# The joined last two attention layers: one order of TensorE by blocks of four heads, four shared PSUM banks, stacks made four heads at a time

## What is computed

```python
# layer 2: 16 heads of 16, keys and values from the normalised context
a = layernorm(ctx) * gamma + beta
Q, K, V = x @ Wq.T, a @ Wk.T, a @ Wv.T
attn = softmax(where(mask, Q K^T * 16 ** -0.5, -inf))
x = x + tanh(gate) * ((attn V) @ Wo.T)
# layer 3: 32 query heads of 8 on 8 key heads, then a layer norm
q, k, v = x @ Wq + bq, ctx @ Wk + bk, ctx @ Wv + bv
attn = softmax(q k^T * 8 ** -0.5 + mask)
x = layernorm((attn v) @ Wo + bo + x) * gamma + beta
```

## Time and profile before

| | us |
|---|---|
| median of three runs | 1309.61 (1308.80 to 1310.96) |
| the profiled execution, timed | 1311.66 |
| its span in the profile | 1309.9 |
| layers 0 and 1, within the span | 0 to 945 |
| layers 2 and 3 | 945 to 1309.9 |

### The profile page before, as it was taken

One profiled execution on the slowest core, in us unless ns is written; L12 is line 12 of the kernel. 1 busy time (PEld: TensorE's weight loads), 2 busy tenths in 40 slices (PEclk: granted clock), 3 DMA queues, 4 the chain that ended last, 5 costly groups with the idle time before them and its releaser, 6 DMA issues. The chain is left out here.

```text
span 1309.9 us, 20641 instructions
## 1 busy us (share of the span) xinstructions
PE 1165.3 (89%) x7388; PEld 897.3 (68%) x7388; DVE 831.0 (63%) x2027; ACT 634.9 (48%) x1420; POOL 678.7 (52%) x735
## 2 busy tenths in 40 slices
PE   5999999999999999999989669874788888899996
PEld 4788888888888888888878624433554556566664
DVE  6776666766757666667666456985554445566764
ACT  3655655555655555555652215103244444566663
POOL 3665665657655665566753032850136433456664
PEclk9999999999999999999999879997889999999999
DMA  6210221102211122102202000000010000000000
GB/s 204 65 49 17 65 65 52 58 21 65 66 49 39 44 65 65 48 18 65 65 17 80 17 0 1 1 0 1 22 43 26 2 1 1 1 2 10 2 10 17
DMA packets 35109, 47.04 MB, mean 36 GB/s; under 512 B 3865, under 2 KB 22082, under 8 KB 35010
## 3 DMA queue, kind: packets, MB, share of 16 engines
q1 hardware_dynamic: 34640, 44.83, 10.8%
q10 hardware_dynamic: 370, 0.91, 0.2%
HBM read 44.69 MB, written 1.05 MB: 35 GB/s over the span
## 5 line engine op out<-in xcount | busy, mean ns | idle before, releaser
L444 POOL TENSOR_TENSOR a_prob<-a_prob,a_inv_total 128x512 f32<-128x512 f32 x128 | 144.1, 1126 | 208.3 <-DVE a_inv_total L732 208.3
L1962 POOL TENSOR_TENSOR scores<-scores,neg_max 128x512 f32<-128x512 f32 x144 | 147.7, 1040 | 160.5 <-DVE neg_max L1833 160.5
L637 ACT ACTIVATE a_prob<-psum,a_neg_max 128x257 f32<-128x257 f32 x256 | 118.9, 472 | 94.1 <-DVE a_neg_max L729 93.3
L1758 ACT ACTIVATE prob_T<-psum 128x512 f32<-128x512 f32 x192 | 110.2, 591 | 75.7 <-PE psum L1677 75.2
L1677 PE MATMUL psum<-ident,scores 128*128 128x128 f32 x768 | 116.9, 285 | 9.8 <-POOL scores L1962 8.2
L1677 PEld LDWEIGHTS psum<-ident,scores 128*128 128x128 f32 x768 | 85.7, 144 | 47.3 <-issue 22.9
L1833 DVE CUSTOM_DVE_ANT_0 scores<-psum,ctx_rows 128x256 f32<-128x256 f32 x256 | 93.0, 419 | 25.6 <-PE psum L1661 25.4
L736 DVE TENSOR_TENSOR a_probT_lo<-psum,a_probT_hi 128x512 fp32r<-128x512 f32 x128 | 88.0, 687 | 32.6 <-ACT a_probT_hi L641 32.1
L566 PE MATMUL psum<-ident,a_prob 128*128 128x128 f32 x512 | 77.8, 274 | 24.0 <-DVE a_probT_lo L736 21.6
L566 PEld LDWEIGHTS psum<-ident,a_prob 128*128 128x128 f32 x512 | 60.0, 140 | 44.6 <-issue 20.8
L729 DVE TENSOR_REDUCE a_neg_max<-psum 128x2 f32<-128x514 f32 x128 | 87.2, 681 | 1.2 <-PE psum L486 1.2
(11 more groups left out here) (348 smaller groups left out, 3349.4 us busy)
## 6 DMA issues: line engine op xcount, KB each, us to landing
wk_raw<-in_L_xattn_wk SPq DMA_DIRECT2D x16, 512.0 KB, 6.5
wq_raw<-in_L_xattn_wq SPq DMA_DIRECT2D x16, 512.0 KB, 5.7
wv_raw<-in_L_xattn_wv SPq DMA_DIRECT2D x16, 512.0 KB, 3.7
wo_raw<-in_L_xattn_wo SPq DMA_DIRECT2D x16, 512.0 KB, 3.9
ctx_rows<-in_ctx SPq DMA_DIRECT2D x3, 512.0 KB, 4.4
x_rows<-in_x SPq DMA_DIRECT2D x2, 512.0 KB, 9.6
ctx_rows<-in_mask_Bx1xSxS_ff SPq DMA_DIRECT2D x1, 1024.0 KB, 5.6
out_dram<-x_rows SPq DMA_DIRECT2D x4, 256.0 KB, 2.1
```

Of the source, the lines that this page charges most:

```text
L444: pool.tensor_tensor(prob[:, m % 4, :, 0:S], prob[:, m % 4, :, 0:S], rtot[:, m % 4, :].unsqueeze(2).to_broadcast([P, 2, S]), ALU.mult)
L637: act.activation(prob[:, m % 4, q, 0:S + 1], s_bank(g)[:, q, 0:S + 1], ACT.Exp, bias=negm[:, m % 4, q:q + 1], accum_out=tot[:, m % 4, q:q ...
L1758: act.activation(pT[:, i % PT, :], t_bank(i), ACT.Exp, scale=1.0 if on_scalar(i) else -1.0).then_inc(exp_ok, 1)
L1962: pool.tensor_tensor(sc[:, i % SC, :, :], sc[:, i % SC, :, :], m[:, i % SC, :].unsqueeze(2).to_broadcast([P, 2, S]), ALU.subtract).then_in ...
```

## The change

- TensorE takes four turns (each with its piece), then two pairs of scores, then the sums of the four heads before: T F T F T F T F S S A. The pairs are those of heads i + 5 to i + 8, so the scores run up to eight heads ahead.
- Turns, sums and pieces share banks 4 to 7 in a ring, in the order of their use; each waits for whoever read that bank before (`bank_read`).
- Stacks are made for four heads at a time (`stack_pieces`), and a block's scores wait only for the stacks of their four heads. The opening ahead of the first scores holds two of them; the others, and the V pieces, stand behind turns. The places of all pieces change; in layer 3 they are two in four turns, later one in three.
- The eviction of the piece behind turn i stands after the maximum of head i + 3 (`LEAD`). The stacks of layer 3's second slot are all evicted by ScalarE.
- The keep of the sums comes one block later. The scale of layer 2's Q is applied in its eviction, and GpSimd no longer scales the weight. GpSimd's side work is cut smaller and spread; its scale and offset of finished rows are two steps, two heads apart.

```diff
+LEAD = 3
-F_BANK = 7
...
-def slot_pieces(l, h):
-    sh = SMALL[l]
-    return ([('Q', l, h, c) for c in range(NC)] + [('K', l, h, c) for c in range(sh.KC)] + [('V', l, h, n) for n in range(2 if l == 2 else 1)]
-            + [('SQ', l, h, g) for g in range(sh.G)] + [('SK', l, h, g) for g in range(8)])
+def stack_pieces(l, h, g):
+    return [('SQ', l, h, g), ('SK', l, h, g)] + ([('SK', l, h, 4 + g)] if l == 2 else [])
...
-    opening = [('XT2', 0, c) for c in range(NC)] + [('CT', 0, c) for c in range(NC)] + [('Q', 2, 0, c) for c in range(NC)]
-    opening += [('XT2', 1, c) for c in range(NC)] + [('AT', 0, c) for c in range(NC)] + [('K', 2, 0, c) for c in range(NC)]
-    opening += [('SQ', 2, 0, g) for g in range(4)] + [('SK', 2, 0, g) for g in range(8)]
-    second = [('V', 2, 0, 0), ('V', 2, 0, 1), ('AT', 1, 0), ('AT', 1, 1)]
+    opening = [('XT2', 0, c) for c in range(NC)] + [('CT', 0, c) for c in range(NC)] + [('Q', 2, 0, 0)] + [('AT', 0, c) for c in range(NC)]
+    opening += [('Q', 2, 0, 1), ('K', 2, 0, 0)] + stack_pieces(2, 0, 0) + stack_pieces(2, 0, 1)
+    second = [('XT2', 1, 0), ('XT2', 1, 1), ('AT', 1, 0), ('AT', 1, 1), ('K', 2, 0, 1)]
     behind = {}
...
-    put(0, [('CT', 1, c) for c in range(NC)] + [('Q', 2, 1, c) for c in range(NC)] + [('K', 2, 1, c) for c in range(NC)]
-        + [('SQ', 2, 1, g) for g in range(4)] + [('SK', 2, 1, g) for g in range(8)] + [('V', 2, 1, n) for n in range(2)])
-    put(20, output_pieces(2, 0) + [('XT3', 0), ('K', 3, 0, 0)])
-    put(28, [('SK', 3, 0, g) for g in range(7)])
-    put(35, output_pieces(2, 1) + [('XT3', 1), ('SK', 3, 0, 7)] + [('Q', 3, 0, c) for c in range(NC)]
-        + [('SQ', 3, 0, g) for g in range(8)] + [('V', 3, 0, 0)])
...
+    put(0, stack_pieces(2, 0, 2) + [('V', 2, 0, 0), ('V', 2, 0, 1)] + stack_pieces(2, 0, 3))
+    put(8, [(kind, 2, 1, c) for kind in 'QK' for c in range(NC)] + [('CT', 1, 0), ('CT', 1, 1)] + stack_pieces(2, 1, 0) + stack_pieces(2, 1, 1))
+    put(20, stack_pieces(2, 1, 2)[:1] + output_pieces(2, 0) + [('XT3', 0)] + stack_pieces(2, 1, 2)[1:] + stack_pieces(2, 1, 3) + [('V', 2, 1, 0), ('V', 2, 1, 1)]
+        + [('K', 3, 0, 0), ('SK', 3, 0, 0)])
+    put(36, [('SK', 3, 0, 1)] + output_pieces(2, 1) + [('XT3', 1), ('Q', 3, 0, 0), ('Q', 3, 0, 1), ('SQ', 3, 0, 0), ('SQ', 3, 0, 1), ('V', 3, 0, 0)]
+        + stack_pieces(3, 0, 2) + stack_pieces(3, 0, 3)[:1])
+    put(53, output_pieces(2, 2) + [('XT3', 2)] + stack_pieces(3, 0, 3)[1:] + [p for g in range(4, 8) for p in stack_pieces(3, 0, g)])
+    put(69, output_pieces(2, 3) + [('XT3', 3), ('K', 3, 1, 0), ('Q', 3, 1, 0), ('Q', 3, 1, 1)]
+        + [(kind, 3, 1, g) for kind in ('SK', 'SQ') for g in range(8)] + [('V', 3, 1, 0)] + output_pieces(3, 0), 2)
+    put(134, output_pieces(3, 1), 3)
+    put(165, output_pieces(3, 2) + output_pieces(3, 3)[:2], 3)
-    bank = {p: k % 8 for k, p in enumerate(opening)}
-    bank.update(zip(second, (7, 6, 4, 5)))
-    bank.update({p: F_BANK for p in behind.values()})
-    bank.update(zip(ending, (7, 0, 1, 2)))
-
-    pe = [('F', p) for p in opening] + [('S', 0), ('S', 1)] + [('F', p) for p in second]
+    pe = [('F', p) for p in opening] + [('S', 0), ('S', 1)] + [('F', p) for p in second] + [('S', 2), ('S', 3)]
     for i in range(HEADS):
         pe.append(('T', i))
         if i in behind:
             pe.append(('F', behind[i]))
-        if i % 2 and i // 2 + 2 < HEADS // 2:
-            pe.append(('S', i // 2 + 2))
-        if i % 4 == 1 and i > 4:
-            pe.append(('A', i // 4 - 1))
+        if i % 4 == 3:
+            pe += [('S', s) for s in (i // 2 + 3, i // 2 + 4) if s < HEADS // 2]
+            if i > 4:
+                pe.append(('A', i // 4 - 1))
     pe += [('A', QUADS - 1)] + [('F', p) for p in ending]
+
+
+    bank, earlier, held, ring = {}, {}, {}, 0
+    for kind, p in pe:
+        if kind != 'S':
+            if kind == 'F' and p in opening:
+                b = opening.index(p) % 8
+            else:
+                b = 4 + ring % 4
+                ring += 1
+            bank[kind, p], earlier[kind, p] = b, held.get(b)
+            held[b] = (kind, p)
...
-        if kind == 'S' and p == 1:
+        if kind == 'S' and p == 2:
             act.append(('shift', 2))
         if kind == 'T':
             at = p
             act.append(('exp', p))
+            if p % 4 == 0 and p > 4:
+                act.append(('keep', p // 4 - 2))
         if kind == 'A' and p == QUADS - 1:
             at = HEADS
-            act.append(('keep', p))
+            act += [('keep', p - 1), ('keep', p)]
         if kind == 'F':
-            if p == ('SQ', 2, 0, 0):
+            if p == ('V', 2, 0, 0):
                 act.append(('gate', 0))
-                dve.append(('mask', 0))
             if evictor(p) == 'act' or p[0] in 'QK':
                 act.append(('E', p))
             if evictor(p) == 'dve':
-                if p[0] == 'V' and p[1:3] == (2, 0):
-                    max_to(1 + p[3])
+                if p == ('K', 2, 0, 1):
+                    max_to(1)
                 elif at >= 0:
-                    max_to(at + 2)
+                    max_to(at + LEAD)
                 dve.append(('E', p))
-                if p == ('Q', 2, 0, 1):
-                    dve.append(('normalise', 1))
+                if p == ('Q', 2, 0, 0):
+                    dve += [('mask', 0), ('normalise', 1)]
                 if p[:2] == ('OP', 3):
                     dve.append(('moments', p[2]))
             if at % 4 == 3 and at + 3 < HEADS:
                 act.append(('shift', at + 3))
-            if at % 4 == 2 and at > 4:
-                act.append(('keep', at // 4 - 1))
-    return pe, act, dve, bank, behind
+    return pe, act, dve, bank, earlier, behind
...
     if p[0] in ('SQ', 'SK'):
-        return 'act' if p[3] % 2 == 0 else 'dve'
+        return 'act' if p[3] % 2 == 0 or p[1:3] == (3, 1) else 'dve'
...
+                def bank_read(use):
+
+                    if earlier[use]:
+                        kind, what = earlier[use]
+                        if kind == 'F':
+                            landed(pe, [what])
+                        else:
+                            pe.wait_ge(exp_ok if kind == 'T' else kept, what + 1)
...
-                    if s == 0:
-                        landed(pe, [p for p in number if number[p] < number['V', 2, 0, 0]])
-                    elif e == 0 and b % 2 == 0:
-                        landed(pe, slot_pieces(l, b // 2))
+                    if s < 2:
+                        pieces = [p for (kind, p), bank in bank_of.items() if kind == 'F' and bank < 4]
+                        landed(pe, [max((p for p in pieces if evictor(p) == who), key=number.get) for who in ('act', 'dve')])
+                    if e % 4 == 0 and b % 2 == 0:
+                        landed(pe, stack_pieces(l, b // 2, e // 4))
...
-                    if i < 2:
-                        landed(pe, [('AT', 1, i)])
-                    else:
-                        pe.wait_ge(exp_ok, i - 1)
+                    bank_read(('T', i))
...
-                            act.activation(dst, src[0:r, :], ACT.Copy).then_inc(hi_ok, 1)
+                            act.activation(dst, src[0:r, :], ACT.Identity, scale=-SMALL[2].scale if kind == 'Q' else 1.0).then_inc(hi_ok, 1)
...
                 def extras(i):
+                    if i == 4:
+                        set_ones(2, 1).then_inc(ones, 1)
+                    if i == 6:
+                        clear(spare[1].bitcast(F32))
                     if i == 8:
                         pool.wait_ge(ld['q3'], 16)
                         pool.tensor_scalar(w3['q'][:, :, :], w3['q'][:, :, :], -SMALL[3].scale, None, ALU.mult).then_inc(scaled, 1)
+                    if i == 10:
                         pool.tensor_scalar(nq[:, :].unsqueeze(2), chip.vecs[:, :, VROWS['L3_xattn_bq']:VROWS['L3_xattn_bq'] + 1], -SMALL[3].scale, None, ALU.mult).then_inc(bias_ok, 1)
-                    if i == 12:
-                        pool.wait_ge(ld['mask3'], 16)
-                        pool.tensor_scalar(mask3[:, 0:4, :], mask3[:, 0:4, :], -1.0, None, ALU.mult)
-                    if i == 14:
-                        pool.tensor_scalar(mask3[:, 4:8, :], mask3[:, 4:8, :], -1.0, None, ALU.mult).then_inc(mask_ok, 1)
-                    if i == position['V', 2, 1, 1] + 3:
-                        made(pool, ('V', 2, 1, 1))
+                        clear(selq[3][:].rearrange("p a g j r w -> p (a g j r w)").bitcast(F32))
+                    for k in range(4):
+                        if i == 12 + 2 * k:
+                            choose_keys(k)
+                        if i == 24 + 2 * k:
+                            choose_queries(k)
+                        if i == 40 + 3 * k:
+                            pool.wait_ge(ld['mask3'], 16)
+                            two = mask3[:, 2 * k:2 * k + 2, :]
+                            pool.tensor_scalar(two, two, -1.0, None, ALU.mult).then_inc(mask_ok, 1)
```

(53 more changed lines are left out.)

45 lines of the change are left out of this document (23 added, 22 removed).

## The result

The changed kernel is slower: 1327.5 us median (1320.9 to 1328.32) against 1309.84 (1308.8 to 1310.96) for the kernel before on the same chip, a ratio of 1.0128 with a 95% interval of 1.0097 to 1.0159. Forecast were 1297.8, and at most 1319. Its profiled execution took 1320.9 us, span 1318.9.

A forecast was written before the change was run, and what follows sets the result against it. TensorE's order was taken as the limit. Turn 0 at 966.3 plus blocks of 317.4 gave last sums at 1283.7 against 1295.47, 11.8 us less; from a median of 1309.61 that made 1297.8 us, range 1268 to 1319.

The forecast's parts named there:

- The opening: Ahead of turn 0: fewer pieces and no scaling of Wq put turn 0 at 966.3, 11.1 us earlier.
- rival 3: Half-clock stretch and VectorE's queue hold the first scores: turn 0 at 975, 1307 to 1310 us, no change; chance 0.09.
- The waits that go: TensorE's waits for bank 7's eviction (9.0 us) and GpSimd's subtraction (8.2 us) vanish, not counted beside the blocks.
- The ring: Banks 4 to 7 shared by turns, sums and pieces: turns' waits for their bank costed at nothing.
- The chain: Heads' blocks: second pair waits for a maximum behind VectorE's evictions; all blocks sum to 317.4 us against 318.0 before.
- OP: Layer 3 blocks with this piece: eviction, moments, GpSimd's power and normalisation precede the last maximum; 10.2 us, 12.0 with an OT.
- OT behind two turns: Blocks with this piece behind turns 1 and 3: 6.06 us against a TensorE sum of 4.5.
- Q, Q, K, K: Layer 2 block with these four pieces: last ends at 8.7, then evictions, a maximum, second pair and sums; 12.7 us.
- Rival 2: Half clock after waits in half of 32 chained blocks, 1.24 us each: 20 us more, 1318; chance 0.19 including longer chains.
- The median: Whole kernel: median of the runs taken as 2.05 us below the profiled execution.
- Changes between transposes and scores: TensorE's blocks: four turns, then two pairs together, save 0.6 us per four heads of 4.15, 29 us over 48 blocks unwaited.
- Rival 1: TensorE binds in the heads, second pair hardly waits: 259.5 us of blocks, 1240, or 1269 with half; chance 0.16.

The follow-up runs named there:

- filled kernel: Changed kernel with idle identity transposes between the two pairs of scores in seven blocks (groups of four: 3, 3, 4, 4, 5, 5, 9): 1320.83 us, ratio 1.0106.
- lead of five: Changed kernel with LEAD raised from 3 to 5, maxima never beyond the pairs already issued: 1252.29 us, ratio 0.9575.

## Why the prediction was wrong

- **The opening: right in kind, its last digit by luck.** Turn 0 at 966.3 forecast, 966.32 measured, and rival 3 (975) is out. But the forecast was 964.7 at full clock and 1.6 us for half clock. The clock up to turn 0 was full (1.00), and what took its place is a wait that the sum did not have: the fourth pair stands 2.12 us for a maximum (965.66). With the same opening turn 0 stood anywhere from 964.04 to 968.46 in the other runs.
- **The waits that go: right.** The waits of the stack pieces for k_stack's eviction and of the turns for GpSimd went from 17.2 us to 0.2. The ring, costed at nothing as to waits of the turns, shows none; its worth was never priced by itself, since the blocks were summed whole.
- **The chain: right in kind, a little short in size.** Blocks 2 to 47 were forecast at 301.0 us. Away from half clock most came within 0.6: OP 10.2 and 10.52 (its two waits 1.93 and 2.67 us, forecast at 4 to 5 together), OT behind two turns 6.1 and 6.18, unchained 4.6 and 4.56, the first two blocks up to their sums 15.5 and 15.3. Q, Q, K, K (12.7) took 14.3, and 13.9 in the filled kernel, though in both the sums ahead of it ran at half clock, and blocks 13 and 17 1.2 us more than forecast each. All such shortfalls make about 10 of the 21 us that the profiled execution was above its forecast (322.0 against 301.0).
- **The clock: the step that failed.** Rival 2 named the mechanism and its sign, with 1.24 us a place and sixteen places for 20 us. It came with fewer and dearer places: seven to ten half-clock sums, and 0.7 to 2.7 us for each of the six places that were filled. 11.2 us of the 21 are shown by the filled kernel, and 8.1 more separate the two executions of the same program. The clock granted over the heads was 0.94 and 0.92 in the two, against 0.97 before. The error was in how the sums were set against each other. The 318.0 us of the kernel before are a measured time and hold five half-clock sums, among them; the 317.4 of the changed one were put together from rows at full clock, but for the earlier trace rows, though each chained block held an idle stretch of the kind that the earlier trace rows follows. The Trainium skill (TensorE: Matmul & The Clock Gate, "A second HAM failure mode: psum-queue depth-cycling") says that frequent short idling between groups makes the clock swing; the trace agrees, with sums of 1.07 and of 1.9 us for the same 16 matmuls. Weighing it as a rival of 0.19 while leaving it out of the likeliest sum was the mistake.
- **The median: wrong by 8.7 us.** The sum was made against the profiled execution, and the median was taken to lie 2.05 below, as before. It lies 6.6 above. The changed kernel has executions with more and with fewer half-clock places, and its runs spread from 1318 to 1328. The runs of before that stood beside it (1309 to 1311) gave no hint of that; later ones, beside the experiments, spread from 1305 to 1314.
- **Changes between transposes and scores: over-priced.** 0.6 us a block were forecast; blocks without pieces went from 4.15 to 3.75, those with two stack pieces from 4.84 to 4.56, so 0.3 to 0.4. The price of a long run of scores was taken from the earlier trace rows, whose 1.25 us for 16 matmuls lie in a stretch at half clock (granted 0.50 from 968.0 to 974.8); at full clock the changed kernel takes 0.87. The four turns in a row cost more than forecast instead (2.20 us against 1.88 with the turn to the scores). The Trainium skill (TensorEngine Tiling (Array Packing), Key Properties) says that a change of tiling mode drains TensorE and gives no time for it; the trace agrees that fewer changes save time, but at the lead of three the waits outweigh it.
- **Rival 1** (TensorE binds, 1240 to 1269) was refuted for the changed kernel, and is what the lead of five reaches: 1252.3.

What the 29.7 us between 1297.8 and 1327.5 are made of, then: 11 in the clock of the profiled execution (shown block by block with the wait held fixed), some 10 that are left, for the most part chains that are longer than forecast, and 8.7 between that execution and the median (that it is the clock too is shown block by block for one pair of executions; for the other runs only their mean granted clock says so). Without the price of the six places the changed kernel's profiled execution would have taken about 1309.7 us, as an estimate (1320.9 less 11.2), 2 less than that of before with its five half-clock sums: the forecast gain of 11.8 would not have come even then. Left open is what makes TensorE fall to half clock after one wait of 1.3 us and not after the next; no run here tells it.

## What to carry to other kernels

When one engine's instructions are grouped, look at what each wait in the group needs and where that stands in the other engine's written order: here the second pair of a block asks for the maximum of head 4k+7, four to seven heads ahead of the block's turns, while VectorE was told to be only three ahead of a turn before its eviction, and one number, held to the pairs already issued, repaired it (1327.5 to 1252.3 us). Price old and new on the same footing: if the measured time of before holds stretches at half clock, a sum for after that is made of full-clock rows is a lower end, not the likeliest value. Check at which clock each of those rows ran, too. Where waits multiply, allow the median to lie above the profiled execution, and look for an order in which the wait is covered or never arises before pricing it.

## What the runs showed of the hardware

- Two executions of one program differ by 8.1 us in 330 through TensorE's granted clock (0.94 and 0.91), with blocks alike within 0.02 us where it did not fall: the same block after the same wait of 1.3 us took 6.18 us or 7.81.
- With TensorE kept busy by idle transposes through a wait, the sums behind it ran at full clock at all six places (1.07 in place of 1.94 us), but at one of them the transposes themselves fell to half clock (3.74 in place of 2.40 us), and three other places fell that had been at full clock: of 11.2 us gained 7.6 were given back.
- A second pair of scores (32-row tiles) costs 0.28 us a block more when transposes stand between the two pairs, and 0.41 when sums do, in blocks where nothing waits (4.84 and 4.97 against 4.56).
